# Layer 2 of a four-layer graph kernel: scores and tanh one step earlier, and a new order of VectorE's and TensorE's work

## The reference

```python
def _L2_gnn_ref(h, adj, W, bW, attn, A_w, fc_w, g1_w, g2_w, gbias):
    Wh = jnp.einsum('bni,hoi->bhno', h, W) + bW[None, :, None, :]
    e = jnp.einsum('bhno,hop->bhnp', Wh, attn)
    scores = jnp.einsum('bhnp,bhmp->bhnm', e, Wh)
    A_mat = jnp.tanh(jnp.where(adj[:, None, :, :], scores, 0.0))
    hp = jax.nn.relu(jnp.einsum('bhnm,bhmo->bhno', A_mat, Wh))
    cat = jnp.transpose(hp, (0, 2, 1, 3)).reshape(hp.shape[0], hp.shape[2], -1)
    ha = cat @ A_w.T
    hf = h @ fc_w.T
    coeff = jax.nn.sigmoid(hf @ g1_w.T + ha @ g2_w.T + gbias)
    return hf * coeff + ha * (1.0 - coeff)
```

## Time and profile before

| | us |
|---|---|
| median of 3 runs | 1870.46 |
| lowest, highest | 1868.22, 1870.58 |
| the profiled execution, its own time | 1872.48 |
| its span, first to last instruction | 1870.5 |
| mean granted TensorE clock in it | 0.986 |

### The profile page before, as it was taken

One profiled execution on the slowest core, in us unless ns is written; L12 is line 12 of the kernel. 1 busy time (PEld: TensorE's weight loads), 2 busy tenths in 40 slices (PEclk: granted clock), 3 DMA queues, 4 the chain that ended last, 5 costly groups with the idle time before them and its releaser, 6 DMA issues. The chain is left out here.

```text
span 1870.5 us, 73862 instructions
## 1 busy us (share of the span) xinstructions
PE 1816.5 (97%) x30736; PEld 1711.1 (91%) x30736; DVE 1272.1 (68%) x2892; ACT 897.1 (48%) x1997; POOL 690.1 (37%) x876
## 2 busy tenths in 40 slices
PE   7999999799999899999999999999999889999998
PEld 7899999799999799999999999999999889999997
DVE  6777777577777455655556555565555479999997
ACT  6677777466666433333333333333333245555554
POOL 3566666243433210000000000000000068998897
PEclk9999999899999999999999999999999989999998
DMA  3223222443333301101111010110010022222222
GB/s 109 88 75 85 86 81 74 128 134 103 86 101 88 95 25 36 36 26 33 29 34 34 26 31 29 34 34 29 29 29 29 19 60 72 69 69 81 74 69 64
DMA packets 149457, 113.63 MB, mean 61 GB/s; under 512 B 43008, under 2 KB 148864, under 8 KB 149376
## 3 DMA queue, kind: packets, MB, share of 16 engines
q1 hardware_dynamic: 149376, 112.46, 20.6%
HBM read 78.87 MB, written 33.55 MB: 60 GB/s over the span
## 5 line engine op out<-in xcount | busy, mean ns | idle before, releaser
L281 POOL TENSOR_TENSOR ln_rstd<-ln_var_eps,minus_half 128x2 f32<-128x2 f32 x128 | 91.3, 713 | 912.9 <-DVE ln_var_eps L274 910.2
L188 PE MATMUL banks<-ln_hT_hi,l_g_w_hi 128*128 128x256 f32 x512 | 148.7, 290 | 6.5 <-PEq L378 3.3
L188 PE MATMUL banks<-ln_hT_hi,square_w_hi_held 128*128 128x256 f32 x512 | 150.1, 293 | 4.4 <-DVE square_w_lo_held L669 3.2
L299 ACT ACTIVATE ln_h<-ln_x,ln_shift,ln_rstd 128x256 f32<-128x256 f32 x256 | 140.1, 602 | 20.6 <-DVE ln_shift L288 20.6
L1836 ACT ACTIVATE l_cat_hi<-banks 128x512 fp32r<-128x512 f32 x128 | 66.2, 603 | 171.0 <-PE banks L2040 171.0
L188 PE MATMUL banks<-l_cat_hi,l_aw_hi 128*128 128x256 f32 x512 | 145.3, 284 | 2.3 <-DVE l_cat_lo L1909 2.3
L189 PE MATMUL banks<-ln_hT_lo,square_w_hi_held 128*128 128x256 f32 x512 | 143.9, 281 | 0.0
L190 PE MATMUL banks<-ln_hT_hi,square_w_lo_held 128*128 128x256 f32 x512 | 143.8, 281 | 0.0
L190 PE MATMUL banks<-ln_hT_hi,l_g_w_lo 128*128 128x256 f32 x512 | 142.6, 279 | 0.0
L189 PE MATMUL banks<-ln_hT_lo,l_g_w_hi 128*128 128x256 f32 x512 | 142.3, 278 | 0.0
L189 PE MATMUL banks<-l_cat_lo,l_aw_hi 128*128 128x256 f32 x512 | 142.3, 278 | 0.0
(11 more groups left out here) (220 smaller groups left out, 6299.1 us busy)
## 6 DMA issues: line engine op xcount, KB each, us to landing
hidden<-y SPq DMA_DIRECT2D x96, 256.0 KB, 2.1
ln_x<-hidden SPq DMA_DIRECT2D x96, 256.0 KB, 2.7
x_res<-hidden SPq DMA_DIRECT2D x96, 256.0 KB, 2.9
ln_x<-x SPq DMA_DIRECT2D x32, 256.0 KB, 2.8
x_res<-x SPq DMA_DIRECT2D x32, 256.0 KB, 3.0
out<-y SPq DMA_DIRECT2D x32, 256.0 KB, 2.1
l_adj_u<-adj SPq DMA_DIRECT2D x96, 16.0 KB, 2.3
l_stage_attn<-L_attn SPq DMA_DIRECT2D x4, 256.0 KB, 3.1
```

What stands on the lines that cost most here:

```text
L188: nc.tensor.matmul(out, lhs(lh), rhs(rh), start=start, stop=False, skip_group_check=True)
L281: self.nc.gpsimd.tensor_tensor(self.rstd[:, g.slot], self.var_eps[:, g.slot], self.core.minus_half[:, 0:PAIRS], ALU.pow).then_inc(self.rst ...
L299: last = self.nc.scalar.activation(self.h[:, u, p, :], self.x[:, u, p, :], ACT.Relu, bias=self.shift[:, u, p:p + 1], scale=self.rstd[:, u, ...
```

## The change

1. **PE's order.** A step is now G0 to G3, Wh0, hp(c2), scores(b1), Wh1 to Wh5, transposes of yT(e), transposes of ln_h(gn), ha, hf, gate. The scores are those of b1, one step earlier than before, and follow hp. Ahead of hp, PE also waits until all four gT of b1 are out (`g_ready`, with `apart`).
2. **Wh.** `UNITS` begins with the two units of 260 columns, which hold tanh's bias columns; a unit of 512 columns is computed as two of 256 in the same bank.
3. **ACT.** tanh is that of b1 and comes behind cat_hi and ln_h.
4. **DVE.** The mask (c2) comes first in the step; the four gT follow the blend directly, and then the statistics and variance; the shift comes behind two of cat_lo; y(e) comes behind the low part of ln_hT.
5. **POOL and SP.** The root (L281) comes last in POOL's step. SP issues the four loads of aw behind the first load of x.
6. **Banks.** Scores move from bank 4 to bank 0 (shared with the transposes of ln_h, which now wait for tanh), the transposes of yT from 0 to 4.
7. **End of layer 1.** ACT splits wh_w behind the loop over G's weights and in two pieces; DVE takes the first half of wh_w_lo, POOL the second alone.

```diff
         for k in range(CH):
             h, jc = divmod(k, KC)
-            if k == 6:
-                act.wait_ge(self.wh_w_loaded.sem, 16 * KC)
-                nc.scalar.activation(self.wh_w_hi[:, :, 0:HD], self.wh_w[:], ACT.Copy).then_inc(self.wh_w_split.sem, 1)
...
             nc.scalar.activation(self.wh_w_hi[:, jc, HD + h:HD + h + 1], ps[:, self.bank(k), D:D + 1],
                                  ACT.Copy).then_inc(self.g_hi.sem, 1)
+        act.wait_ge(self.wh_w_loaded.sem, 16 * KC)
+        for c in range(KC):
+            nc.scalar.activation(self.wh_w_hi[:, c, 0:HD], self.wh_w[:, c], ACT.Copy).then_inc(self.wh_w_split.sem, 1)
...
                                     self.wh_w_hi[:, jc, HD + h:HD + h + 1], ALU.subtract).then_inc(self.g_used.sem, 1)
+        dve.wait_ge(self.wh_w_split.sem, 1)
+        nc.vector.tensor_tensor(self.wh_w_lo[:, 0, 0:HD], self.wh_w[:, 0], self.wh_w_hi[:, 0, 0:HD], ALU.subtract)
...
     def split_wh_w_lo(self, pool):
 
-        pool.wait_ge(self.wh_w_split.sem, 1)
-        for c in range(KC):
-            self.core.nc.gpsimd.tensor_tensor(self.wh_w_lo[:, c, 0:self.H * D], self.wh_w[:, c],
-                                              self.wh_w_hi[:, c, 0:self.H * D], ALU.subtract)
+        pool.wait_ge(self.wh_w_split.sem, KC)
+        self.core.nc.gpsimd.tensor_tensor(self.wh_w_lo[:, 1, 0:self.H * D], self.wh_w[:, 1],
+                                          self.wh_w_hi[:, 1, 0:self.H * D], ALU.subtract)
...
-    UNITS = ((0, 0, 512), (1, 0, 512), (0, 512, 256), (0, 768, WC - 768), (1, 512, 256), (1, 768, WC - 768))
+    UNITS = ((0, 768, WC - 768), (1, 768, WC - 768), (0, 0, 512), (1, 0, 512), (0, 512, 256), (1, 512, 256))
...
-        B_HT = B_YT = 0
+        B_HT, B_YT = 0, 4
         B_G, B_WH, B_HF = (1, 2, 3, 1), (2, 3, 1, 2, 3, 1), 2
-        B_GATE, B_S = 3, 4
+        B_GATE, B_S = 3, 0
...
-            for k in range(0, CH, KC):
-                sp.dma_start(aw[:, k:k + KC], rows(w["AwT"])[:, k:k + KC]).then_inc(weights.aw_loaded.sem, 16)
...
                 if gn is not None:
                     ln.load(sp, gn)
+                if g.reg is None and g.c == 0:
+                    for k in range(0, CH, KC):
+                        sp.dma_start(aw[:, k:k + KC], rows(w["AwT"])[:, k:k + KC]).then_inc(weights.aw_loaded.sem, 16)
...
-                if gn is not None:
-                    ln.root(pool, gn)
...
                     nc.gpsimd.tensor_scalar(adj[:, b1.slot], adj_u8[:, b1.slot], 1.0, None,
                                             ALU.mult).then_inc(adj_ready.sem, 1)
+                if gn is not None:
+                    ln.root(pool, gn)
...
                 if c2.exists(groups):
-                    known(act, a_pool_ready, c2.back(1))
-                    known(act, a_dve_ready, c2.back(1))
-                    after(act, wh_ready, c2)
-                    after(act, scores_in_psum, c2)
+                    known(act, ha_in_psum, c2.back(1))
+                    for i in range(H):
+                        round_hp(i)
+                if gn is not None:
+                    ln.apply(act, gn)
+                if b1.exists(groups):
+                    known(act, a_pool_ready, b1.back(1))
+                    known(act, a_dve_ready, b1.back(1))
+                    after(act, wh_ready, b1, 2)
+                    after(act, scores_in_psum, b1)
...
                     last.then_inc(th_ready.sem, 1)
-                if c2.exists(groups):
-                    known(act, ha_in_psum, c2.back(1))
-                    for i in range(H):
-                        round_hp(i)
-                if gn is not None:
-                    ln.apply(act, gn)
...
                     after(dve, wh_in_psum, b1, i + 1)
                     if i == 0:
-                        known(dve, hp_in_psum, b1.back(1), 2)
-                    if i == 2:
-                        known(dve, hp_in_psum, b1.back(1))
+                        after(dve, hp_in_psum, b1.back(1))
                     nc.vector.tensor_tensor(wh[:, p, c0:c0 + n], ps[:, B_WH[i], 0:n], wh_bias[:, c0:c0 + n],
...
+                if c2.exists(groups):
+
+                    after(dve, adj_ready, c2)
+                    after(dve, th_ready, c2)
+                    known(dve, hp_in_psum, c2.back(1))
+                    nc.vector.tensor_tensor(a[:, :, HEADS_OF_DVE], th[:, :, HEADS_OF_DVE],
+                                            adj[:, c2.slot].unsqueeze(2).to_broadcast([P, PAIRS, 2, S]),
+                                            ALU.mult).then_inc(a_dve_ready.sem, 1)
                 if e.exists(groups):
...
-                if gn is not None:
-                    ln.statistics(dve, gn, first=True)
-                if c2.exists(groups):
-
-                    after(dve, adj_ready, c2)
-                    after(dve, th_ready, c2)
-                    known(dve, hp_in_psum, c2.back(1))
-                    nc.vector.tensor_tensor(a[:, :, HEADS_OF_DVE], th[:, :, HEADS_OF_DVE],
-                                            adj[:, c2.slot].unsqueeze(2).to_broadcast([P, PAIRS, 2, S]),
-                                            ALU.mult).then_inc(a_dve_ready.sem, 1)
-                if gn is not None:
-                    ln.statistics(dve, gn, first=False)
                 if b1.exists(groups):
                     evacuate_g(0)
                     evacuate_g(1)
-                if e.exists(groups):
-                    after_dma(dve, x_res_loaded, e)
-                    after_dma(dve, y_stored, e.back(2))
-                    after(dve, yT_in_psum, e)
-                    nc.vector.tensor_tensor(y[:, e.slot], ps[:, B_YT, :].rearrange("q (p d) -> q p d", p=PAIRS),
-                                            x_res[:, e.slot], ALU.add).then_inc(y_ready.sem, 1)
                 if b1.exists(groups):
                     evacuate_g(2)
                     evacuate_g(3)
                 if gn is not None:
-                    ln.shifts(dve, gn)
+                    ln.statistics(dve, gn, first=True)
+                if gn is not None:
+                    ln.statistics(dve, gn, first=False)
                 if c2.exists(groups):
                     split_hp(0)
                     split_hp(1)
+                if gn is not None:
+                    ln.shifts(dve, gn)
+                if c2.exists(groups):
                     split_hp(2)
                 if b1.exists(groups):
                     evacuate_wh(0)
...
                 if gn is not None:
                     known(dve, scores_in_psum, gn.back(2))
                     ln.evacuate_lo(dve, gn, B_HT)
+                if e.exists(groups):
+                    after_dma(dve, x_res_loaded, e)
+                    after_dma(dve, y_stored, e.back(2))
+                    after(dve, yT_in_psum, e)
+                    nc.vector.tensor_tensor(y[:, e.slot], ps[:, B_YT, :].rearrange("q (p d) -> q p d", p=PAIRS),
+                                            x_res[:, e.slot], ALU.add).then_inc(y_ready.sem, 1)
...
-                if c2.exists(groups):
-                    u = c2.slot
-                    known(pe, g_ready, c2, apart=core)
-                    if first_products(g.back(1)):
-                        pe.wait_ge(next_weights.made.sem, next_weights.SMALL_MADE)
-                    known(pe, th_ready, c2.back(1), apart=core)
+                def scores():
+
+                    u = b1.slot
...
                     last.then_inc(scores_in_psum.sem, 1)
+
+                def product_wh(i):
+                    p, c0, n = UNITS[i]
+
+                    if i < 3:
+                        after(pe, g_ready, b1, i + 2)
+                    else:
+                        after(pe, wh_ready, b1, i - 2)
+                    for k, w in ((0, D), (D, D)) if n == 2 * D else ((0, n),):
+                        for c in range(KC):
+                            last = mm3(nc, ps[:, B_WH[i], k:k + w], hT, (wh_w_hi, wh_w_lo), c == 0, c == KC - 1,
+                                       lambda t: t[:, c, p * P:(p + 1) * P], lambda t: t[:, c, c0 + k:c0 + k + w])
+                    last.then_inc(wh_in_psum.sem, 1)
+
                 if b1.exists(groups):
                     known(pe, ln.hT_hi_ready, b1)
                     after(pe, ln.hT_lo_ready, b1)
                     product_g(0)
                     product_g(1)
+                if b1.exists(groups):
+                    product_g(2)
+                    product_g(3)
+                    product_wh(0)
+                    after(pe, g_ready, b1, apart=core)
...
+                    after(pe, a_dve_ready, c2, apart=core)
+                    after(pe, a_pool_ready, c2, apart=core)
+                    product_hp()
+                if b1.exists(groups):
+                    scores()
+                    for i in range(1, 6):
+                        product_wh(i)
                 if e.exists(groups):
                     after(pe, blend_steps, e)
-                    known(pe, ln.hT_lo_ready, e.back(-2))
```

(14 more changed lines are left out.)

24 lines of the change are left out of this document (7 added, 17 removed).

## The result

The changed kernel takes 1894.58 us (median of 4 runs, 1890.30 to 1897.16), the kernel before 1870.16 beside it (4 runs, 1868.22 to 1870.58). The ratio is 1.0124, with a 95% interval of 1.0110 to 1.0139. The forecast was 1871.3, in a range of 1862 to 1877. It was wrong: the kernel is 24.4 us slower.

The account below looks back on a forecast made before the run. PE's own work and the drains between its forms were taken to bound layer 2's loop; -4.7 (loop) + 0.1 (written-out steps) + 3.1 (start) + 0.7 (end) = -0.8 us, a loss, giving 1871.3 us, range 1862 to 1877.

Parts of the forecast that it names:

- 2.03 and 2.01 around the scores: Loop step: 2.03 us from hp's start to the scores, 2.01 from the scores to the next form; 0.20 saved.
- 0.02 for the transposes: Loop step: transposes of yT next to those of ln_h save one exit, 0.02 us, between 0 and 0.1.
- 0.08 for the split: Loop step: computing 512-column matmuls as two halves saves 0.08 us.
- the wait ahead of hp: Loop step: PE waits for the last gT, then three wait instructions; 0.45 us lost, between 0.09 and 0.5.
- t + 1.01: Loop step, t being the start of G3's last matmul: the last gT was forecast out at t + 1.00.
- the first rival: Ahead of hp: waits behind g_ready cost nothing, PE restarts about 0.05 after gT; 1862.7 us, chance 0.22.
- 0.03 for G3: Loop step: G3 needs the first gT out; 0.03 us lost, between 0 and 0.1.
- two ordinary distances of 0.114: Loop step: matmul spacing subtracted from the 2.45 us between gate and G, leaving 2.22 us for the scores.
- Start of layer 2: Layer 2's first steps: 3.2 us stall and clock loss go, scores are added; 3.1 us gained (1.5 to 4.5).
- End of layer 2: Layer 2's last steps: 1.86 us gained, 0.4 lost to transposes, 0.75 to clock; 0.7 gained (-0.6 to 1.5).
- The blend becomes the bound: Ahead of G3: the chain gate, tanh, blend, gT 0 comes late; 1880.6 us at 0.3 a step, chance 0.12.
- a period above 26.3: Loop: sign that the blend's chain bounds the step, seen as PE waiting ahead of G3; forecast period 26.1.

Follow-up runs that it names:

- e2: Kernel before with yT's transposes moved directly ahead of those of ln_h, their result in bank 4: 1868.98 us, 0.9998.
- e3: Kernel before with each 512-column Wh unit computed as two products of 256 columns: 1869.30 us, 0.9997.
- e9: Changed kernel with the last transpose of yT done twice, nine transposes in a row instead of eight: 1891.38 us, 1.0113.
- e17: Changed kernel with one extra, overwritten matmul of 288 columns at the head of the ha product's second half: 1889.88 us, 1.0102.
- e4: Changed kernel with the split of the 512-column Wh units taken back: 1891.02 us, 1.0108.
- e11: Changed kernel with both 260-column units ahead of hp, the last Wh unit 260 columns wide, and 512-column units undivided: 1878.39 us, 1.0037.
- e8: Changed kernel with both 260-column units ahead of hp and the last Wh unit 260 columns wide: 1867.60 us, 0.9973.

## Why the prediction was wrong, point by point

**The loop step was worked out from the right rows, but at a pace that it took for given.** Every distance of the working is there: 2.03 and 2.01 around the scores; 0.02 for the transposes (e2); 0.08 for the split (e3). One term was too small: the wait ahead of hp. The last gT is out at t + 1.01, as forecast. hp starts 0.45 behind it in the loop and 0.06 in the written-out steps, where the first rival had 0.05. So the three waits that are instructions of their own cost 0.39, and with the passing of the semaphore 0.45, where the forecast made both 0.36 of the earlier trace rows. hp restarts 0.73 behind its neighbour where it took 0.21: 0.52 lost a step against 0.45 forecast, beyond the bound of 0.5. The 0.03 for G3 didn't show in the changed kernel. Without pace and halts the steps lost 5.8 us against 4.0; 26 times the 0.07 is 1.8 us, the size of that difference. The step that failed is "two ordinary distances of 0.114" and its like: the prediction took the 113.3 ns of layer 2 for the price of a matmul in any order. It is one of two. The 168 matmuls of 256 columns in a step by 4.6 ns are 0.8 us when all are slow; 0.6 us a step, 18.2 in all, came in this way. Why the new order falls to the slow pace the runs don't show. No rival had it, and the range had no room for it.

**The trace of before had the second pace in it.** Up to 640 us, in layers 0 and 1, 1381 distances of its 256-column matmuls are at 116 to 119 ns and 1328 at 113 to 115. Layer 2's loop was almost wholly at the fast pace, 3981 to 408. Someone who asks why the same kind of instruction takes 118 ns in one layer and 113 in the next would have given the change a rival: "the new order loses the fast pace, 31 x 0.6 to 0.8 = 18 to 25 us slower". Being nearly all at the better of two levels, the kernel had little to gain there and much to lose.

**Start of layer 2: right.** Up to the first hp 4.7 us are gained, where the forecast's terms give 4.4 by that mark. The stall went, and the clock stays up, where the earlier trace rows had 0.76 and 0.59:

```profile
650.00:660.00 10.00, 9.93 (x132) 9.66 (x132) 6.38 (x13) 4.91 (x14) 5.89 (x6) 1.00 0.31 90
```

**The loop's first pass: not thought of.** The two halts of 1.3 and 1.5 us by the profile's count (3.2 us by the distances of the matmuls) stand in the two steps of the loop's first pass. Here is the second, in PE's timeline, and the row on instruction loads from 809 to 813 us:

```profile
809.04 1.96 PE L2040 MATMUL banks<-l_a,l_wh 64*64 64x64 f32 x117 [0.45 <-DVE l_gT L1893]
812.46 0.45 PE L2040 MATMUL banks<-l_a,l_wh 64*64 64x64 f32 x11 [1.46 <-issue]
```

```profile
q8 instruction: 1, 0.02, 1.4%
```

From 840 us on the trace has no such load in the loop, and no halt. hp and the scores are now 192 small matmuls in a row, which use up instructions faster than anything else in the step. That PE ran out of them fits, but it was only argued: the kernel before has such loads in the same steps without a halt, and e9 and e17, which keep that order, had no halt either. In e3, e4 and e11 halts of 0.6 to 1.0 us stand in written-out steps. What is measured is a loss of 0 to 3.5 us that comes and goes with small edits.

**End of layer 2: the waits came, the clock was underpriced.** Forecast 0.7 gained: 1.86 ahead of the last hp, less 0.4 and 0.75 behind it. Measured: from the gate's last matmul to the last hp are 3.60 us instead of 5.36, 1.76 gained, and behind hp 1.7 are lost against 1.15. That leaves 0.1 gained, inside the bounds of -0.6 and 1.5. PE stands idle for 3.32 us ahead of the last hp and for 2.10 behind it (before 1.20 and 2.33), and hp itself then took 3.69 us at half clock instead of 2.10:

```profile
1503.55 3.69 PE L2040 MATMUL banks<-l_a,l_wh 64*64 64x64 f32 x128 [3.32 <-DVE l_yT L1932]
1509.34 1.08 PE L2097 MATMUL banks<-constants_sb,l_yT 128*128 128x128 f32 x4 [2.10 <-DVE l_cat_lo L1908]
```

```profile
1503.50:1511.90 8.40, 6.25 (x140) 6.12 (x141) 3.27 (x5) 2.17 (x4) 0.00 (x0) 0.50 0.01 2
```

The term that was too small is the clock: 0.75 was taken for hp, 1.6 were lost there. The transposes of yT behind it took 0.74, where the forecast had 0.4. The ha product behind them is at the lower level for its first 11 distances, but before it was so for 14, as the kernel before shows:

```profile
1486.00:1488.00 2.00, 2.00 (x12) 2.00 (x11) 0.00 (x0) 0.00 (x0) 0.00 (x0) 0.50 0.00 0
```

From its first matmul to the gate's first it takes 7.98 us instead of 8.35, which gives 0.4 back. PE's shorter idle time behind hp gives another 0.2.

**The rivals.** "The waits behind g_ready cost nothing" is refuted for the loop by 0.45 in 26 steps, and holds in the written-out ones (0.06). "The blend becomes the bound" is refuted too: no row of the changed kernel has PE waiting ahead of G3, and e8, at the fast pace, has 0.02. The sign that I named for it, a period above 26.3, came without it.
